# An attention and feed-forward block: the probability blocks packed two sequences by two heads, and the conditioning matrices picked by four products

## The reference

```python
w = weights[subjects]                       # subjects: 32 numbers below 31; weights: 32 x 32 x 32
h = einsum('bct,bcd->bdt', x, w)            # conditioning: each sequence by its own 32 x 32 matrix
q, k, v = h @ wq.T, h @ wk.T, h @ wv.T      # 32 heads of 16, rotary on q and k
scores = q @ k.T / 4, causal in 32 x 32;  attn = softmax(scores)
x = x + (attn @ v) @ wo.T
y = x @ W.T + 2 * sum over the two best of 8 experts of gate * (x @ A[e].T) @ B[e].T
y = y[:, perm];  y = gelu(y per 16 heads of 32 @ up) @ down;  y = y[:, unperm]
out = x + y
```

## Time and profile before

| what | value |
|---|---|
| median of 3 runs | 212.55 us (211.69 to 213.61) |
| profiled execution, its own time | 214.02 us |
| its span in the trace | 212.2 us |
| TensorE busy | 203.5 us (96%) |
| VectorE, ScalarE, GpSimd busy | 148.0, 119.2, 119.2 us |
| mean granted clock of TensorE | 0.984 |

### The profile page before, as it was taken

One profiled execution on the slowest core, in us unless ns is written; L12 is line 12 of the kernel. 1 busy time (PEld: TensorE's weight loads), 2 busy tenths in 40 slices (PEclk: granted clock), 3 DMA queues, 4 the chain that ended last, 5 costly groups with the idle time before them and its releaser, 6 DMA issues.

```text
span 212.2 us, 6020 instructions
## 1 busy us (share of the span) xinstructions
PE 203.5 (96%) x2548; PEld 176.2 (83%) x2548; DVE 148.0 (70%) x287; ACT 119.2 (56%) x209; POOL 119.2 (56%) x93
## 2 busy tenths in 40 slices
PE   7799999999989999999999999999999999798993
PEld 5699987988769899986779899886698987688863
DVE  4897799999749877837619788546678995258123
ACT  2491465279763445289744454399755777533460
POOL 8263999699770203978982113969978253524000
PEclk9859999999999999999999999999999999999999
DMA  6999602005001330000062420000135200224002
GB/s 198 383 395 375 206 3 103 0 5 197 3 5 47 102 99 3 2 5 0 0 67 38 123 78 3 0 3 2 12 41 127 26 3 3 24 28 49 0 3 99
DMA packets 9930, 15.18 MB, mean 72 GB/s; under 512 B 1328, under 2 KB 5680, under 8 KB 9904
## 3 DMA queue, kind: packets, MB, share of 16 engines
q1 hardware_dynamic: 7440, 11.37, 15.6%
q0 software_dynamic: 2048, 2.88, 8.4%
q10 hardware_dynamic: 416, 0.55, 0.8%
HBM read 11.13 MB, written 3.67 MB: 70 GB/s over the span
## 4 chain that ended last, share of the span: by engine, by line
PE 89%; DVE 4%; ACT 3%; issue 1%; DMA 1%; ACTq 0%; DVEq 0%
PE ps_A L624 11%; PE ps_F L624 10%; PE ps_A L626 10%; PE ps_A L625 10%; PE ps_F L625 9%; PE ps_F L626 9%; PE ps_S L778 5%; PE ps_F L868 5%; PE ps_S L883 3%; PE ps_S L756 3%; PE ps_A L681 2%; PE ps_A L778 1%; PE ps_A L896 1%; ACT pbd L1056 1%; DMA y<-in_ids 1%
## 5 line engine op out<-in xcount | busy, mean ns | idle before, releaser
L570 POOL TENSOR_TENSOR pr<-pr,small 128x512 f32<-128x512 f32 x16 | 17.6, 1110 | 38.8 <-DVE small L1419 38.6
L1056 ACT ACTIVATE pbd<-pr 32x512 f32<-32x512 f32 x56 | 35.2, 629 | 1.3 <-DVE pr L1425 0.6
L550 POOL DMA_INDIRECT out<-y,row_at x12 | 19.8, 1647 | 11.4 <-ACT y L1056 8.9
L1117 ACT ACTIVATE pr<-pr 128x512 f32<-128x512 f32 x16 | 10.1, 633 | 24.4 <-DVE pr L1411 24.3
L507 POOL TENSOR_TENSOR rot<-rot,cst 128x512 f32<-128x512 f32 x11 | 14.4, 1305 | 15.9 <-DVE rot L1377 15.9
L1161 ACT ACTIVATE act<-ps_F 128x512 f32<-128x512 f32 x32 | 16.5, 603 | 11.3 <-PE ps_F L868 11.3
L1397 DVE TENSOR_TENSOR kbd<-kr,cst 128x512 f32<-128x512 f32 x13 | 18.9, 1486 | 3.0 <-POOL kr L511 3.0
L520 POOL TENSOR_TENSOR kbd<-kr,cst 128x512 f32<-128x512 f32 x15 | 19.4, 1320 | 0.1
L624 PE MATMUL ps_F<-x,w2T 128*128 128x256 f32 x56 | 16.1, 287 | 0.0
L626 PE MATMUL ps_F<-x,w2T 128*128 128x256 f32 x56 | 15.6, 279 | 0.0
L625 PE MATMUL ps_F<-x,w2T 128*128 128x256 f32 x56 | 15.6, 279 | 0.0
(11 more groups left out here) (237 smaller groups left out, 662.8 us busy)
## 6 DMA issues: line engine op xcount, KB each, us to landing
xt<-in_xT SPq DMA_DIRECT2D x4, 512.0 KB, 4.1
xs<-in_x SPq DMA_DIRECT2D x3, 512.0 KB, 8.0
out<-xt SPq DMA_DIRECT2D x3, 512.0 KB, 3.1
act<-in_L_attn_wk SPq DMA_DIRECT2D x1, 1024.0 KB
act<-in_L_attn_wv SPq DMA_DIRECT2D x1, 1024.0 KB
act<-in_L_attn_wo SPq DMA_DIRECT2D x1, 1024.0 KB, 7.1
xs<-in_x ACTq DMA_DIRECT2D x1, 512.0 KB, 5.1
pr<-in_L_attn_wq SPq DMA_DIRECT2D x2, 256.0 KB, 4.8
```

The costliest lines, as they stand in the source:

```text
L550: pool.indirect_dma_start(out=out, out_offset=bass.IndirectOffsetOnAxis(ap=row_at[:, g, c:c + 1], axis=0), in_=y[:, c, :], in_offset=None, ...
L570: pool.tensor_tensor(pr[:, i, :, :], pr[:, i, :, :], mx[:, i, :].unsqueeze(2).to_broadcast([P, NH // 2, T]), ALU.mult).then_inc(normed, 1)
L1056: return sc.activation(dst, src, ACT.Copy)
```

## The change

It alters three things. PV: `pbd` and `vz` are laid out anew. The 128 rows of a product are now two heads (k) by two sequences by 32 keys, and its 64 columns two sequences by 32 queries; s says which two sequences. `pv` still makes eight products for each c, now of 64 columns and each complete in itself. To fill the rows, `probs_block` makes eight copies of 32 rows by 256 instead of four of 32 by 512, each to rows and columns of its own, `probs_half` likewise, and `v_out` four copies of 64 rows by 256 instead of one of 128 by 512. Conditioning: one `onehot` of 128 rows, four products of 128 rows by 32 columns by 256 into one bank, one transpose. The start: x of group 0 is loaded by SyncE's queue as its second transfer instead of by ScalarE's queue; `onehots` no longer waits for the constants (TensorE does, and `biases`); five and three idle products instead of six and four; `pbd` is zeroed by four ScalarE copies after `blocks(1)`, in place of two GpSimd memsets ahead of `perm_rows`.

```diff
-        wsel = sb("wsel", [P, T, T])
+        wsel = sb("wsel", [P, SC, BT, TILES])
-        vz = sb("vz", [P, 3, NH // 2, 3 * HD])
+        vz = sb("vz", [P, 3, NH // 2, 2, 2 * HD])
-        pbd = sb("pbd", [P, 2, NH // 2, BT, T])
+        pbd = sb("pbd", [P, 2, HC, 2, 2 * T])
...
+        def pairs_of(tile, b, k):
+            rows = P // 2 * k + T * (b % 2)
+            return tile[rows:rows + T, :, b // 2, T * (b % 2):T * (b % 2) + T]
+        def heads_of(turned_half, b, k):
+            return turned_half[T * b:T * b + T, :, :].rearrange("p (q k) t -> p q k t", k=2)[:, :, k, :]
...
             sp.dma_start(cst[:, 0:EARLY], consts[:, 0:EARLY]).then_inc(d_cst, 16)
+            load_x(0)
...
         def probs_half(i):
...
                 for b in range(2, BT):
-                    at = slice(T * b, T * b + T)
-                    pool.tensor_copy(pbd_of(G - 1, 1, i)[at, :, b, :], pT(2 + i)[at, :, :]).then_inc(pbd_p, 1)
+                    for k in range(2):
+                        pool.tensor_copy(pairs_of(pbd_of(G - 1, 1, i), b, k), heads_of(pT(2 + i), b, k)
+                                         ).then_inc(pbd_p, 1)
-            for i in range(2):
-                pool.memset(pbd[:, i, :, :, :], 0.0).then_inc(pbd_zero, 1)
...
-            def select(r):
-                rows = slice(T * r, T * r + T)
+            def select():
                 for j in range(BT):
                     at = slice(T * j, T * j + T)
-                    last = pe.matmul(bank(it)[at, 0:SC * T], onehot[rows, at], wst[rows, :],
+                    last = pe.matmul(bank(it)[at, 0:SC * T], onehot[:, at], wst[:, :],
...
         def pv(g, t, c):
-                for e in range(2):
+                for s in range(2):
+                    at = P * c + P // 2 * s
                     for j in range(4):
-                        last = pe.matmul(bank(it)[32 * j:32 * j + 32, P * c:P * c + P],
-                                         vz_of(g, t)[:, 4 * c + j, HD * e:HD * e + 2 * HD],
-                                         pbd_of(g, t, c // 2)[:, HC * (c % 2) + 2 * j + e, :, :],
-                                         start=(e == 0), stop=(e == 1), skip_group_check=True)
+                        last = pe.matmul(bank(it)[32 * j:32 * j + 32, at:at + P // 2], vz_of(g, t)[:, 4 * c + j, s, :],
+                                         pbd_of(g, t, c // 2)[:, HC // 2 * (c % 2) + j, s, :],
+                                         start=True, stop=True, skip_group_check=True)
...
             pe.wait_ge(zero_ready, 1)
-            idle_products(6, rings["S"][0])
+            idle_products(5, rings["S"][0])
+            pe.wait_ge(d_cst, 16)
             pe.wait_ge(onehot_ready, 1)
-            for r in range(BT):
-                select(r)
-            idle_products(4, rings["S"][0])
+            select()
+            idle_products(3, rings["S"][0])
...
         def v_out(g, t):
-                dst = vz_of(g, t).rearrange("p q (s f) -> p q s f", f=HD)[:, :, 0:3:2, :]
-                copy(dst, bank(it)[:, :].rearrange("p (q s f) -> p q s f", s=2, f=HD)).then_inc(s_free(it), 1)
+                heads = bank(it)[:, :].rearrange("p (q k f) -> p q k f", k=2, f=HD)
+                for s in range(2):
+                    for k in range(2):
+                        last = copy(vz_of(g, t)[P // 2 * k:P // 2 * k + P // 2, :, s, HD * k:HD * k + HD],
+                                    heads[P // 2 * s:P // 2 * s + P // 2, :, k, :])
+                last.then_inc(s_free(it), 1)
...
         def probs_block(g, t, i):
                 for b in range(BT):
-                    at = slice(T * b, T * b + T)
-                    last = copy(pbd_of(g, t, i)[at, :, b, :], pT(2 * t + i)[at, :, :])
+                    for k in range(2):
+                        last = copy(pairs_of(pbd_of(g, t, i), b, k), heads_of(pT(2 * t + i), b, k))
...
-            sc.dma_start(xs[:, 0, :, :], x_d[0]).then_inc(d_x[0], 16)
...
             blocks(1)
+            sc.wait_ge(vz_zero, 1)
+            for i in range(2):
+                for h in range(2):
+                    copy(pbd[:, i, HC // 2 * h:HC // 2 * h + HC // 2, :, :].rearrange("p q s k -> p (q s k)"),
+                         vz[:, 0, 0:HC, :, :].rearrange("p q s f -> p (q s f)")).then_inc(pbd_zero, 1)
             w_his("wo", raw["wo"], WT["wo"], (d_w["wo"], None))
...
             def onehots():
                 ve.wait_ge(d_ids, 16)
-                ve.wait_ge(d_cst, 16)
...
-            for r in range(BT):
-                turn_selected(r)
+            turn_selected()
```

More of the change, by code:

```diff
@@ L155, in ropes_to @@
             return 4 * g + i if g else min(i + 1, 3)
-        kbd_pbd = [kbd[:, i, :, :, :].rearrange("p c b k -> p (c b k)").rearrange("p (h b t) -> p h b t", b=BT, t=T)
-                   for i in range(2)]
+        kbd_pbd = [kbd[:, i, :, :, :].rearrange("p c b k -> p (c b k)")[:, 0:HC * 4 * T].rearrange(
+            "p (q s k) -> p q s k", q=HC, s=2) for i in range(2)]
         def pbd_of(g, t, i):
@@ L253, in f_fill @@
                 F_AT[name] = len(F_AT)
-        f_fill(*(("sel", r) for r in range(BT)), ("Q", 0), ("Q", 1), ("K", 0), ("K", 1), ("scores", 0),
+        f_fill(("sel",), ("Q", 0), ("Q", 1), ("K", 0), ("K", 1), ("scores", 0),
                ("scores", 1))
@@ L493, in _ @@
         def _(pool):
-            pool.memset(vz[:, 0:2, :, :], 0.0).then_inc(vz_zero, 1)
+            pool.memset(vz[:, 0:2, :, :, :], 0.0).then_inc(vz_zero, 1)
             def perm_rows():
@@ L528, in kbd_zeros @@
                 wait_full(pool, S_scores(G - 1, 2 * t + 1))
-                pool.memset(kbd[:, t, :, :, :], 0.0).then_inc(kbd_zero, 1)
+                pool.memset(kbd_pbd[t], 0.0).then_inc(kbd_zero, 1)
             def wo_half(h):
@@ L540, in third_v @@
                 wait_full(pool, prep("w2", KC - 1))
-                pool.memset(vz[:, 2, :, :], 0.0).then_inc(vz_zero, 1)
+                pool.memset(vz[:, 2, :, :, :], 0.0).then_inc(vz_zero, 1)
             def add_rows(g, *cs):
@@ L559, in probs_half @@
                 if i:
-                    pool.wait_ge(pbd_p, 2 * i)
+                    pool.wait_ge(pbd_p, 4 * i)
                 pool.wait_ge(turned, 4 * (G - 1) + i + 3)
@@ L605, in _ @@
                     probs_half(1)
-                    pool.wait_ge(pbd_p, 4)
+                    pool.wait_ge(pbd_p, 8)
                     add_rows(g - 1, 0, 1, 2, 3)
@@ L1108, in v_out @@
                     sc.wait_ge(vz_zero, g + 1)
+                    if g == 0:
+                        sc.wait_ge(pbd_zero, 4)
                 if GT * g + t >= 3:
@@ L1345, in first_cond_lo, with turn_selected @@
                                  ).then_inc(s_free(it), 1)
-            def turn_selected(r):
-                it = Fi("sel", r)
+            def turn_selected():
+                it = Fi("sel")
                 wait_full(ve, it)
-                ve.transpose(wsel[:, SC * r:SC * r + SC, :].rearrange("p d t -> p (d t)"),
+                ve.transpose(wsel[:, :, :, :].rearrange("p d r t -> p (d r t)"),
                              bank(it)[:, 0:SC * T]).then_inc(s_free(it), 1)
             def blocks(g):
-                for r in range(BT):
-                    wait_read(ve, Fi("sel", r))
+                wait_read(ve, Fi("sel"))
                 if g:
@@ L1361, in blocks @@
                 for b in range(2):
-                    i = ve.tensor_scalar(wbd[:, :, b, :], wsel_of(g), con("pair")[:, b:b + 1], None, ALU.mult)
+                    i = ve.tensor_scalar(wbd[:, :, b, :].rearrange("p t (r d) -> p t r d", r=BT), wsel_of(g), con("pair")[:, b:b + 1], None, ALU.mult)
                 i.then_inc(wbd_ready, 1)
@@ L1431, in probs_half @@
                 for b in range(2):
-                    at = slice(T * b, T * b + T)
-                    last = ve.tensor_copy(pbd_of(G - 1, 1, i)[at, :, b, :], pT(2 + i)[at, :, :])
+                    for k in range(2):
+                        last = ve.tensor_copy(pairs_of(pbd_of(G - 1, 1, i), b, k), heads_of(pT(2 + i), b, k))
                 last.then_inc(pbd_v, 1)
@@ L1547, in onehots @@
                 ve.wait_ge(d_ids, 16)
-                ve.wait_ge(d_cst, 16)
[L1549 to L1552, removed]
+                wide = [P, BT, BT, TILES]
+                ve.tensor_tensor(onehot.rearrange("p (j r t) -> p j r t", j=BT, r=BT),
+                                 ids[:, 0:B].rearrange("p (j t) -> p j t", j=BT).unsqueeze(2).to_broadcast(wide),
+                                 matrix_at.unsqueeze(1).unsqueeze(3).to_broadcast(wide), ALU.is_equal
+                                 ).then_inc(onehot_ready, 1)
             def biases():
                 step(ve.tensor_copy(langf, ids[:, B:B + TILES]))
+                ve.wait_ge(d_cst, 16)
                 step(ve.tensor_tensor(bias, con("expert").unsqueeze(1).to_broadcast([P, TILES, E]),
@@ L1715, in laid_out @@
     of_row = np.broadcast_to(a["itok_B_0_30"].reshape(TILES, BT).T.reshape(1, B), (P, B))
```

(4 more changed lines are left out.)

19 lines of the change are left out of this document (10 added, 9 removed).

## The result

| | before | after |
|---|---|---|
| median of 4 runs, us | 212.61 (211.69 to 213.61) | 231.94 (230.70 to 232.28) |
| ratio, 95% interval | 1 | 1.0898 (1.0834 to 1.0961) |
| profiled execution: time, span, us | 214.02, 212.2 | 231.94, 230.1 |
| mean granted clock | 0.984 | 0.933 |

What follows compares the result with a forecast made beforehand. TensorE looked limiting (96% busy), but ScalarE's copies, only 0.15 us ahead, would set the pace. First group with start +1.54, middle groups +4.92, last -0.50: +5.96 us, forecast 218.5 us against 212.55, range 210.5 to 224.

Steps and rivals of the forecast that it cites:

- TensorE's clock falls: Rival: idle TensorE drops to 1.2 GHz, 1.7 to 3.3 us per stretch; one to three give 220 to 228; chance 0.18.
- the idle time: TensorE waiting for ScalarE: 0.8 and 3.3 us in each middle group, about 4 of 5 us in the first.
- the start's gain: Before the first group: matrices ready some 2 us sooner, of which 1.5 us taken (ends 1.3 and 2.6).
- The copies' own cost: ScalarE's added copy time: block +0.81, v_out +1.05 us; +3.04 per middle group before PV's saving, +3.04 net in the first.
- no overlap: ScalarE copies that change source or target rows start 0.42 us apart; 0.32 would be full overlap.
- PV: On TensorE: 32 records with 64 columns take 0.55 us instead of 1.01, 17.0 ns a record.
- The rival that the records stay at 31.5 ns: PV's records bound by their weight loads, no cheaper; sum +1.4 us higher, 219.9 us; chance 0.07.
- Middle groups: Two groups where PV's second half waits for ScalarE's third block: +3.04 less 0.43, +2.46 us each, +4.92 together.
- Last group: Copies on VectorE and GpSimd there; last PV and feed-forward beside it keep 0.5 us (ends 0 and 1.3): -0.5.
- The first group: ScalarE's queue from first block to v_out(1, 1): +3.04 net, less 1.5 us from the start: +1.54 us.
- The first rope: Sign to look for: VectorE's first rope near 17.4 us, where it had started at 18.68.

Runs made afterwards that it cites:

- number 1: Kernel after, with 42 identity products put into TensorE's waits for ScalarE; 220.81 us, ratio 1.0417.
- number 2: Kernel before with only the new start and conditioning, its own PV kept; 211.11 us, ratio 1.000.
- number 8: Number 1 with the old start and conditioning, so PV's change alone with waits filled; 221.05 us, ratio 1.0406.
- number 5: Kernel after with ScalarE's block copies moving neither side's rows within fours, only source, or only target, by group; one execution, 226.14 us.
- number 4: Kernel after with half of the block copies on ScalarE left out (four per block); 211.25 us, ratio 0.9962.
- number 7: Number 1 with two of v_out's four copies left out; 219.16 us, ratio 1.0272.
- number 6: Kernel after, VectorE taking half of three blocks' copies in groups 1 and 2, v_out(1, 1) earlier and waits filled in group 0; 221.68 us, ratio 1.0282.

## Why the prediction was wrong

**The step that failed** stands in the rivals: "TensorE's clock falls", with a chance of 0.18 and a price of 1.7 to 3.3 us a stretch, taken as 222.5 us. The forecast was summed at full speed, and the clock fell at all three places. That cost 3.8, 5.0 and 2.1 us, 10.9 together (number 1 against after, from the first block copy on). The forecast itself had written down the idle time: 0.8 and 3.3 us in a middle group (0.90 us came, then 0.80 and 2.52) and about 4 us in the first (1.88 and 2.18 came). The row beside which it was weighed had 1.49 us idle of 3.40 and was followed by the low clock, and the idle time that was predicted was longer, so the rival deserved more. The price was low as well: the prediction had one stretch of 6.65 us (6.8 in the trace, whose rows were read only up to 15.60), but they lasted 10.2, 13.7 and 6.8 us. The first two ran on into products that fill the engine (`cond` took 3.67 us for 2.00).

**A second term was mis-sized**: the start's gain, 1.5 us in the sum, of which no run shows anything in the time (numbers 2 and 8). The copies' own cost was right to about 1 us of 7.5 (number 1 against number 2).

**What held.**
- Copies: 415 ns (416 forecast) and 0.425 us from start to start (0.42); a block 3.40 (3.36); v_out 1.55 (1.54). Number 5 shows why no overlap was the right choice.
- PV: 32 records of its second half 0.58 us at full clock (0.55), 18 ns a record. It is cheaper, and number 4 shows 1.9 us a group against before, 1.3 against number 2, where nothing takes it back. The rival that the records stay at 31.5 ns is refuted. For the sum it made little, since it lies where TensorE waits.
- Middle groups: +2.7 and +2.6 (+2.46), of which 0.6 is my fill's overrun; `cond` then comes 38.6 us behind the router before it and came after 35.8 in before, +2.9, and 0.2 is given back in `scores`, which had a small gap in before (1.39 us for 60 records). Against number 2's groups they are +3.4 and +3.2, the overrun included.
- Last group: -0.8 (-0.5, upper end 1.3).
- The first group came out +2.1 (+1.54), of two parts. From the first block copy to `cond`, number 1 took 62.29 - 42.40 = 19.9 us for before's 16.6: +3.3 (+3.04). The first block copy began 1.4 us sooner (1.5). But before's execution had the clock at half from 9.0 to 15.8 us and number 1's had not, so that the 1.5 looks right is luck. The first rope began at 17.30 (forecast 17.4).

**What was missed beside the clock.** TensorE also waits for `v_out` indirectly: the eviction of the output projection is queued behind it on ScalarE, VectorE's sum behind that, and the first half of PV behind the sum (0.80 us, "DVE xc", above). The forecast had these only as work queued on ScalarE. It cost nothing by itself here, since the third block is later still, but it is idle time next to the wait of 2.52 us, 3.3 together, and the clock fell in the second of them.

**What stays open.** How much each of the waits contributed to each fall, and why nearly the same waits were followed by 13.65 us at half speed in after and by 3.4 in number 5; the gaps in `scores` of number 7; the 0.6 us by which number 2's middle groups are shorter than before's; and whether any layout of PV's 128 rows with fewer changes of rows in the copies would win. No kernel with the new PV and all its copies came below before; number 6 is 2.8% slower, numbers 1 and 8 are 4% slower, and number 4, which leaves half of the block copies out, is level with before.

## What to carry to other kernels

When a forecast leaves TensorE idle for microseconds ahead of dense work, sum it twice, at both clock levels, and give the lower one a large chance if the kernel's own trace shows a fall after less idle time. Here the clock was 10.9 of the 17.9 us of span lost. It is a chance and no rule: a wait of 1.5 us was followed by a fall in number 4 and by none in numbers 1 and 2. A saving on the engine with 96% busy time is worth nothing where its feeder is only 0.15 us ahead, and splitting the feeder's copies then costs start by start, twice the count at two thirds of the length. To tell lost clock from lost time, fill the waits with products that nobody needs: it is one small edit, and the difference is the clock's. Before reading it, look whether the two executions ran their start at the same clock; here that was 0.5 us, and 3.1 in number 8.

## What the runs showed of the hardware that was not expected

- **Overlap of ScalarE's copies hangs on rows.** Copies of 32 x 256 start 0.305 us apart if source and target keep their rows, and 0.425 apart if either moves (number 5). The Trainium skill ("ScalarE: Activation LUTs", What ACT_TABLE_LOAD costs) gives an overlap of about 93 ns for ACTIVATEs back to back: with the 0.415 us of one copy the first figure is an overlap of 0.11 us and agrees with it, the second is none and doesn't.
- **Low stretches can be long, and their length varies.** 10.2, 13.7 and 6.8 us in after, behind waits of 1.88 and 2.18, of 0.80 and 2.52, and again of 0.80 and 2.52 us. Number 5 had 3.4 us behind 0.79 and 2.52, and number 4 had 3.4 us behind 0.47 and 2.18.
- **The column of the clock begins with 1.00** before its first recorded change. In after, products of 256 columns by threes take 0.64 us until 13.58 and 0.35 from there on, half speed where the stretch 9 to 15 us shows 1.00.
- **VectorE's copies are slow beside GpSimd's instructions.** A copy of 32 x 256 took 0.30 us on VectorE while GpSimd stood still and 1.1 us while it ran, against 0.42 on ScalarE (number 6).
